# Another order at the head of the feed-forward stages and of the expert stages of a two-layer hybrid network

## The reference, cut to what matters

```
def experts(x):                        # x is layer-normed, then added to the residual
    probs = softmax(x @ router.T)      # 8 experts
    weights, indices = top_k(probs, 2); weights /= weights.sum(-1) + 1e-6
    h = silu(x @ w1[e]) * (x @ w3[e])  # hidden 256, for every expert e
    return sum over the two chosen e of weights[e] * (h @ w2[e])
def feed_forward(x):                   # x is layer-normed, then added to the residual
    h = silu((x @ w1) * s1) * ((x @ w2w) * s2)     # hidden 512
    h = gelu((h @ h1) * h1s);  h = gelu((h @ h2) * h2s)
    return (h @ w3) * s3
```

## Time and profile before

| | |
|---|---|
| median of 3 runs | 4477.8 us (4477.5 to 4482.8) |
| the profiled execution | 4475.35 us, of which the span of the instructions 4473.5 us |
| mean granted TensorE clock | 0.825 of 2.4 GHz |
| busy, share of the span | PE 75%, DVE 69%, ACT 48%, POOL 19% |
| expert stages | 766.6 to about 1065 us, and about 1881 to about 2179 us of the span |
| feed-forward stages | 2960.6 to 3222.4 us and 4202.8 to 4464.4 us of the span |

### The profile page before, as it was taken

The page is one execution under the profiler, slowest core; times in us unless marked ns, Lnnn a source line. Parts: engine busy times, 40 slices in busy tenths (PEclk is TensorE's granted clock), DMA queues, the critical chain, the costliest instruction groups (busy, mean ns, idle before and its releaser), DMA issues. The chain is left out here.

```text
span 4473.5 us, 85746 instructions
## 1 busy us (share of the span) xinstructions
PE 3368.7 (75%) x35552; PEld 1534.3 (34%) x35552; DVE 3070.2 (69%) x4612; ACT 2145.0 (48%) x3615; POOL 839.3 (19%) x734
## 2 busy tenths in 40 slices
PE   6999998996556555699779888879845464663699
PEld 1222222563112111256433333324424343442344
DVE  8889895876787787787525677644465858667553
ACT  4888887664533342366422666646431221121364
POOL 1000100552343344455431001010000000000000
PEclk7999999997666576799889999979965666665699
DMA  3101101000110101000261012010000000000000
GB/s 90 25 20 19 25 8 33 2 1 9 29 28 0 29 0 29 29 2 2 36 81 32 11 37 38 23 47 1 12 2 4 2 3 2 3 3 1 27 1 20
DMA packets 138474, 85.31 MB, mean 19 GB/s; under 512 B 94755, under 2 KB 109749, under 8 KB 137957
## 3 DMA queue, kind: packets, MB, share of 16 engines
q1 hardware_dynamic: 135336, 75.56, 8.0%
q0 software_dynamic: 2688, 4.20, 0.6%
q10 hardware_dynamic: 64, 0.07, 0.0%
HBM read 47.81 MB, written 18.60 MB: 15 GB/s over the span
## 5 line engine op out<-in xcount | busy, mean ns | idle before, releaser
L833 DVE TENSOR_REDUCE attn_peak_halves<-attn_ps 128x2 f32<-128x1024 f32 x512 | 601.5, 1218 | 61.2 <-PE attn_ps L664 53.4
L786 ACT ACTIVATE attn_weights<-attn_ps 128x512 f32<-128x512 f32 x1024 | 530.9, 602 | 102.9 <-PE attn_ps L692 102.8
L1333 PE MATMUL mamba_ps<-mamba_stack,mamba_spread 96*128 96x512 bf16 x512 | 206.2, 522 | 285.7 <-DVE mamba_driven L1557 140.3
L1499 POOL TENSOR_TENSOR mamba_out_c<-mamba_states,mamba_c_rep 128x1024 f32<-128x1024 f32 x128 | 321.6, 2512 | 488.1 <-DVE mamba_states L1563 475.6
L2681 DVE TENSOR_REDUCE sparse_peak<-sparse_ps 128x4 f32<-128x1024 f32 x256 | 309.2, 1223 | 134.2 <-PE sparse_ps L2311 132.6
L142 PE MATMUL moe_ps<-moe_xT_halves,moe_w_halves 128*128 128x512 f16 x1536 | 364.5, 384 | 12.4 <-DVE moe_w_halves L1097 9.3
L1080 POOL TENSOR_TENSOR moe_hidden<-moe_exact,moe_hidden 128x512 f16<-128x512 f32 x256 | 296.7, 1163 | 342.1 <-ACT moe_hidden L1064 333.8
L2541 ACT ACTIVATE sparse_weights<-sparse_ps 128x512 f32<-128x512 f32 (+1 forms) x512 | 272.0, 585 | 173.9 <-PE sparse_ps L2378 87.8
L142 PE MATMUL ffn_ps<-ffn_layers,ffn_h_halves 128*128 128x512 f16 x1536 | 339.8, 383 | 14.4 <-ACT ffn_gate L2907 14.4
L692 PE MATMUL attn_ps<-attn_q_stack,attn_k_stack 50*128 50x512 f16 x1024 | 321.1, 385 | 33.4 <-ACT attn_weights L786 7.1
L1563 DVE TENSOR_TENSOR_SCAN mamba_states<-mamba_ps,mamba_driven 128x1024 f32<-128x1024 f32 x128 | 293.1, 2290 | 33.0 <-ACT mamba_ps L1475 16.9
(11 more groups left out here) (461 smaller groups left out, 6134.3 us busy)
## 6 DMA issues: line engine op xcount, KB each, us to landing
mamba_stack<-mamba_parts SPq DMA_DIRECT2D x96, 128.0 KB, 2.4
sparse_factor<-sp_factor SPq DMA_DIRECT2D x24, 256.0 KB, 3.7
sp_halves<-sparse_parts SPq DMA_DIRECT2D x8, 512.0 KB, 3.0
ffn_h<-in_h SPq DMA_DIRECT2D x4, 1024.0 KB, 9.0
attn_q_stack<-attn_halves SPq DMA_DIRECT2D x96, 32.0 KB
attn_k_stack<-attn_halves SPq DMA_DIRECT2D x96, 32.0 KB
attn_halves<-attn_hp SPq DMA_DIRECT2D x8, 384.0 KB, 3.3
attn_q_stack<-attn_peak_rows SPq DMA_DIRECT2D x128, 2.0 KB
```

What stands on the lines that cost most here:

```text
L786: act.activation(weights[:, at % 2, h, :], use.slot, ACT.Exp).then_inc(*key_act.one())
L833: dve.tensor_reduce(peak_halves[:, turn % PEAKS, keys, at:at + 2], use.slot, AX_X, ALU.max).then_inc(*score_dve.one())
L1499: pool.tensor_tensor(out_c[:, n % 6, :], states[:, n % 3, :], c_rep[:, b % 2, :], ALU.mult).then_inc(*product_made.one())
```

## The change

The pieces themselves stay the same; no matmul moves. In both feed-forward stages: `h1` is loaded before the scales; the second chunk's tokens come before the split of `h1`; moments and root of batch 1 go from behind the first gated piece to in front of it (four activation table loads fall away, two in each stage); both halves of apply of batch 1 come in front of the first wide piece instead of around it; and DVE's gated piece makes the product of block m + 1 before the low half of block m. In both expert stages: at the start apply comes before the split of expert 0's weights; a new one-column `silu` ("ready") makes the table load early; and the three routing pieces of the first batch are spread over two units, the last of them behind the split of expert 3's weights.

```diff
 # moe_stage
+        ready = sbuf("ready", [P, 1])
...
         def ahead(j):
             if j < 2:
-                yield from ([("logits", 0), ("raise", 0)], [("choose", 0, n) for n in range(3)])[j]
+                yield from ([("logits", 0), ("raise", 0)], [("choose", 0, 1)])[j]
             if j + 2 < EXPERTS:
                 yield "split", j + 2
...
             yield "root", 0
-            yield "split", 0
             for half in range(HALVES):
                 yield "apply", 0, half
+            yield "split", 0
+            yield ("ready",)
             for half in range(HALVES):
                 yield "turn", 0, half
             yield "split", 1
             for j in range(units + 2):
                 if j < units:
                     yield "up", j, 0
+                if j in (1, 2):
+                    yield "choose", 0, 2 * j - 2
...
+                def make_ready():
+
+                    act.wait_ge(*norm.rooted.at(1))
+                    act.activation(ready[:], norm.std[:, 0:1], ACT.Silu)
...
 # ffn_stage
         def ahead(step, layer):
-            yield from {(0, 0): [("moments", 1, 0), ("moments", 1, 1), ("root", 1)],
-                        (1, 0): [("weights", 3), ("apply", 1, 0)],
-                        (1, 1): [("apply", 1, 1), ("tokens", 2), ("tokens", 3)],
+            yield from {(1, 0): [("weights", 3), ("apply", 1, 0), ("apply", 1, 1)],
+                        (1, 1): [("tokens", 2), ("tokens", 3)],
...
             yield "tokens", 0
+            yield "tokens", 1
             yield "weights", 2
-            yield "tokens", 1
+            yield "moments", 1, 0
+            yield "moments", 1, 1
+            yield "root", 1
             for step in range(CHUNKS + 3):
...
             def _(sp):
-                for n in (0, 1):
+                def load_weights(n):
                     what = shapes[n][0]
                     sp.dma_start(exact_w[what][:], net.dram[what].rearrange("(k i) o -> i k o",
                                                                           i=P)).then_inc(*weights_in[n].dma())
+
+                for n in range(3):
+                    load_weights(n)
                 for n in scale:
                     sp.dma_start(scale[n][:], net.dram[n]).then_inc(*scales_in.dma())
                 sp.dma_start(s3[:, 0, :], net.dram["s3"].partition_broadcast(P)).then_inc(*scales_in.dma())
...
+                for n in range(3, len(shapes)):
+                    load_weights(n)
...
                         dve.scalar_tensor_tensor(exact_sb[:, split % 3, :], b.slot, scale["s2"][:, m:m + 1],
                                                  gate_sb[:, gate % 2, :], ALU.mult, ALU.mult).then_inc(*by_dve.one())
-                        dve.wait_ge(*by_dve.at(b.over))
-                        keep_low(n, c, m)
+                        if m:
+                            keep_low(n, c, m - 1)
+                    dve.wait_ge(*by_dve.at(b.over))
+                    keep_low(n, c, WB - 1)
```

More of the change, by code:

```diff
@@ L1065, in keep @@
                                    ACT.Copy).then_inc(*hidden_high.one())
-                pieces = {"root": lambda b: norm.root(act, b), "split": split, "turn": turn, "raise": raise_,
+                pieces = {"root": lambda b: norm.root(act, b), "ready": make_ready, "split": split, "turn": turn, "raise": raise_,
                           "up": up, "keep": keep}
@@ L2821, in _ @@
                 sp.dma_start(s3[:, 0, :], net.dram["s3"].partition_broadcast(P)).then_inc(*scales_in.dma())
-                for n, (what, _, _) in enumerate(shapes):
-                    if n >= 2:
-                        sp.dma_start(exact_w[what][:], net.dram[what].rearrange("(k i) o -> i k o",
-                                                                              i=P)).then_inc(*weights_in[n].dma())
+                for n in range(3, len(shapes)):
+                    load_weights(n)
             @block.tensor
```

## The result

The changed kernel took 4451.6 us (median of 4 runs, 4447.4 to 4454.6) beside 4480.3 us for the kernel before on the same chip: ratio 0.9932, 95% interval 0.992 to 0.9944. By the ratio that is 30.5 us, with 25 to 36 in the interval, and by the two medians 28.7; 33.4 were forecast. The time lies in the range of 4436 to 4456, and outside the 4441 to 4449 that the prediction gave its likeliest case. A second series of the same two kernels gave 0.9926 (0.9912 to 0.9939). The profiled execution took 4447.4 us with a span of 4445.6; its granted clock is 0.826 (before 0.825).

A forecast was written before the change was run, and what follows sets the result against it. PE bounds the feed-forward stages; in the expert stages it waits for a weight split behind routing. 12.9 + 15.5 + 5 = 33.4 us off 4475.35 gave 4442.0, with 2.4 to the median 4444.4, said as 4445; range 4436 to 4456.

The forecast's parts named there:

- First gate: Second feed-forward stage, first gated pass: gate at 4214.7 instead of 4216.29; bounds 0.2 and 1.6 us earlier, 1.6 taken.
- The cover for the scales: Feed-forward, first gate: scales land behind `h1` near 4212, gate at 4214.7, leaving 2 to 3 us to spare.
- Gated passes: Feed-forward: second pass's first gate 5.5 us behind the first's; in the second stage, wide piece 8.9 us earlier, running 10.4.
- Apply and the third pass: Second feed-forward stage: POOL's `h2` split holds apply's last four tiles until 4231.9; third pass at 4236.8, 12.9 us earlier.
- 2.5 us per stage, 5 for the two: Expert stages: total gain from the earlier first product and the spread routing, with ends of 1 and 4.5.
- The head: Start of the expert stages: reciprocal no longer behind a weight split, PE's first product 1.7 us earlier.
- the shorter wait for the split: Expert stages: PE's wait for the weight split behind the routing falls from 4.67 to 2 to 3.5 us.
- takes part of it back: Expert stages: third routing piece delays the sum into the residual and the next product, reducing the gain; no separate size.
- rival (b): Both stage kinds: smaller gains, gate no earlier, apply held whole, clock falls; 24 us, 4454; chance 0.24.
- Rival (a): Both stage kinds: POOL hinders less, clock stays up, experts 2 x 4; 40 us, 4438; chance 0.20.
- rival (d): Feed-forward: PE stays held behind ACT, only the moments' move counts; 5 us per stage, 4468; chance 0.04.
- (c): Feed-forward first gate: scales landing behind 1 MB hold ACT's and DVE's first gated piece; about 4490; chance 0.02.

The follow-up runs named there:

- e5: The changed kernel with the load of `h1` again behind the loads of the scales; ratio to the kernel before 0.9945.
- e6: The changed kernel with both halves of the `h2` split moved behind the transposes and copies of the second batch's tokens; 4444.7 us, ratio to before 0.9926.
- e1: The kernel before with the new feed-forward stages and the old expert stages; ratio to the kernel before 0.9941.
- e7: The changed kernel without the extra one-column activation that loads the Silu table early in the expert stages; ratio to the kernel before 0.9931.
- e8: The changed kernel with the first batch's three routing pieces together again behind the second unit's first product; ratio to the kernel before 0.9939.
- e11: The changed kernel with the first expert's weight split again ahead of the first batch's apply in the expert stages; ratio to the kernel before 0.9922.
- e9: The changed kernel run again with no edit, to see how stages vary between executions; ratio to the kernel before 0.9926.
- e3: The changed kernel with each low half of a gated pass back directly behind its own product on VectorE; ratio to the kernel before 0.9952.

## Why the prediction came out right

**First gate.** Forecast 11.9 us into the second stage, measured 11.8; 1.6 against 1.7 gained (2.1 to 2.3 in the first stage and in the second pair of profiles), and e5 gives 1.6 for the load alone. No gap stands around the table load: the root ends at 4198.85, the load runs from 4198.87 to 4200.15, the gate starts at 4200.16. The cover for the scales held: the last of the five, issued at 4192.17, landed 4.9 us later, 8.7 us into the stage (forecast 9.2), and ScalarE had no wait for them.

**Gated passes.** Second gate forecast 5.5 behind the first, measured 5.4; wide piece forecast at 18.8, measured 18.86, in 10.52. In the first stage 2981.0 and 2980.67.

**Apply and the third pass.** Apply forecast from 24.1 to 30.0 into the stage, measured 23.65 to 29.55, held by POOL as said (e6 shows it; in all other stages with this order it took 6.97, as one tile more was held); third pass forecast 34.0, measured 33.7, with a wait in the range of 2 to 4. The clock fell in the second stage and stayed in the first, as assumed, but that was luck: behind the same wait of 2.7 the changed kernel's second run has the next wide piece 5.2 us after the third pass in one stage and 6.9 in the other, and of the runs with the same feed-forward code the clock fell in the second stage of e1 and e7 and not in that of e8 and e11. In the first stage the forecast third pass was 0.9 early (33.98 against 34.83), since `h1` landed later there and the gate with it (in e9, where ScalarE had no wait for `h1`, it is 34.07); so 14.2 us in that execution, 15.0 over two, for 15.5.

**Behind that point** nothing moves: from the start of the next wide piece the stages last 207.68 and 216.67 us, the same within 0.02 in all 14 profiles.

**Experts, the mis-sized term.** "2.5 us per stage, 5 for the two" measured 4.5 and 5.3. The head (1.7 forecast, 1.7 measured, e11) and the shorter wait for the split (forecast 2 to 3.5, measured 2.94; e8: 2.0 and 2.7) were right. PE got its weights where the forecast had them, at 792.6 in the times of before (791.7 to 794.0). Wrong was the step that "takes part of it back": behind the split wait the stages last 263.7 to 263.8 us in the changed kernel, where it was 263.8 to 265.2, so the third piece cost PE nothing. The head (1.9 over the four stages of each kernel) and the split wait (4.67 to 2.94) make 3.6 us of the 4.5 and 5.3. The rest is, by the traces, TensorE's clock, which the sum put at nothing here (only the upper end of 4.5 had a part of it). Behind the first product it rises 2.4 us earlier in the first stage and 3.2 in the second, more than the 1.9 of the product. Behind the shorter split wait it comes back sooner: over the 8 us from PE's restart the granted clock was 0.83, 0.69, 0.65 and 0.63 before, 0.79 to 0.81 in the changed kernel, 0.68 and 0.69 in e8. The one stage of before with 0.83 is also the one that lasted 263.8 behind its wait, and it is the stage whose rows the prediction read. The second stage before, and in the changed kernel (stretch, busy time by engine, PEclk, DMA share, GB/s):

```profile
1910.51:1918.51 8.00, 8.00 (x49) 4.93 (x50) 6.15 (x15) 4.53 (x10) 3.27 (x3) 0.69 0.00 1
```

```profile
1908.34:1916.34 8.00, 8.00 (x64) 4.77 (x65) 7.79 (x21) 4.92 (x11) 3.52 (x3) 0.81 0.00 1
```

**The sum** left out that untouched stages vary. The touched stages gave 38.0 instead of 33.4, and the time 30.5 (25 to 36). The near hit of the total is therefore luck in part: the experts were forecast 4.8 us too small, and what the untouched stages gave back went the other way. Mamba's 4 us may be part of it, as said under e9. By the time alone 4451.6 lies nearer to rival (b)'s 4454 than to 4445, but the stages show none of (b)'s smaller gains. Rival (a) was nearer on the experts (2 x 4), and e6 shows its unheld apply; rival (d) falls with the feed-forward stages' 15.0 and 13.2 us, for its 5, and with e3; and (c) falls with the missing wait for scales. The rule of the Trainium skill that descriptors are consumed in ring order on each DMA engine (DMA: Bandwidth & Descriptors, Queues, rings and completion order) is not tested by e5: `h1` is in use 2.3 us later there, but SyncE also issues it 2.4 us later. The prediction's reading of it, that the scales come after the whole of `h1`, went too far. In the changed kernel two of the small scale loads, issued behind `h1` at 4190.65 and 4191.14, landed 4.7 us later, up to 7.5 us into the second stage, and ScalarE could begin with `h1` at 7.7.

## What to carry to other kernels

Read a pipeline's head by the order of each engine's list, not by its busy time: a consumer's low half put one block later, so that VectorE does not wait for ScalarE's high half, was worth 15.5 of 28 us (a lower clock in one stage included), and most of it appeared one pass further on, where the next work of the same engine had been queued. Such shares don't add up: undone one by one, the low half, the moments and the load cost 15.5, 9.6 and 5.6 us, 30.7 together. Place a long POOL instruction where the VectorE instructions beside it feed nobody. And count a changed stage by its own length: the time of the whole program varied by more in the stages that nobody had touched than two of the terms were worth.

## What the runs showed of the hardware

The hold between POOL and VectorE goes both ways. In the changed kernel's first profile POOL's product of 128x512 (`w3` by `s3`) took 1.27 us in the first feed-forward stage and 3.19 in the second, where three low halves of VectorE ran beside it at their usual pace, and the low half behind them took 1.40. One apply tile of 128x128, 0.34 us by itself, was held for 4.10 us beside a 4.11 us split. Not every VectorE instruction is held: two gated products, which read PSUM, took 1.41 us together beside POOL's 4.08 us split of `h1`.

TensorE's clock behind a short wait is not settled by the wait's length: behind 2.65 to 2.66 us it stayed at 2.4 GHz in the first feed-forward stage and fell in the second (e9), behind 3.36, 3.49 and 4.43 it was low, behind 1.77 and 1.90 high. Behind the waits of 2.65 to 3.36 it cost 1.5 to 1.7 us of a pass of eight groups (5.2 against 6.7 to 6.9) where it fell. And a wait costs more than its length: behind PE's wait for a weight split the first 8 us ran at a granted clock of 0.63 to 0.69 in seven of eight stages that waited 4.67 us, and at 0.79 to 0.82 in those that waited 2.94.
